# Attention inside a fused block: the order of the maxima and of the P·V products on TensorE is rewritten

## The reference

```
x = x + tanh(g_xattn) * linear(attn_text + attn_image)      # on layernorm(x)
    q = rms_norm(linear(x)); k = rms_norm(linear(ctx)); v = linear(ctx)
    attention(q, k, v) = softmax(q k^T / sqrt(32)) v         # 16 heads of 32
    # the context has 1344 text rows and 257 image rows; each has its own softmax
x = x + tanh(g_ffn) * (top-2 of 8 experts + shared expert)   # on layernorm(x)
```

## Time and profile before

| | |
|---|---|
| median of 3 runs | 1711.67 us |
| the profiled execution | 1710.61 us |
| its span, first to last instruction | 1709.1 us |
| PE busy | 1667.6 us, 98% of the span |
| DVE busy | 1185.1 us, 69% |
| ACT busy | 833.4 us, 49% |
| POOL busy | 901.4 us, 53% |
| granted TensorE clock, mean | 0.996 |

### The profile page before, as it was taken

The page is one execution under the profiler, slowest core; times in us unless marked ns, Lnnn a source line. Parts: engine busy times, 40 slices in busy tenths (PEclk is TensorE's granted clock), DMA queues, the critical chain, the costliest instruction groups (busy, mean ns, idle before and its releaser), DMA issues. The chain is left out here.

```text
span 1709.1 us, 24784 instructions
## 1 busy us (share of the span) xinstructions
PE 1667.6 (98%) x8694; PEld 1116.5 (65%) x8694; DVE 1185.1 (69%) x2220; ACT 833.4 (49%) x1550; POOL 901.4 (53%) x343
## 2 busy tenths in 40 slices
PE   6999999999999999999999999998999999999999
PEld 5888878886444455555555545445777778888777
DVE  6876677668888887888878888777444454443565
ACT  4443333326666664666556666662221355554221
POOL 3221311215777775788747777710515576775642
PEclk9999999999999999999999999999999999999999
DMA  9556858646555552565555655211314477885532
GB/s 331 169 159 195 241 173 208 197 150 196 152 155 156 146 153 66 154 159 157 139 136 147 158 135 140 93 48 42 136 38 157 167 258 262 269 273 197 174 103 99
DMA packets 198603, 277.34 MB, mean 162 GB/s; under 512 B 30968, under 2 KB 128008, under 8 KB 197964
## 3 DMA queue, kind: packets, MB, share of 16 engines
q1 hardware_dynamic: 192928, 258.91, 51.0%
q0 software_dynamic: 5120, 16.78, 2.9%
q10 hardware_dynamic: 432, 0.07, 0.0%
HBM read 202.21 MB, written 106.42 MB: 181 GB/s over the span
## 5 line engine op out<-in xcount | busy, mean ns | idle before, releaser
L1294 ACT ACTIVATE P<-ps 128x512 f32<-128x512 f32 (+1 forms) x832 | 445.2, 597 | 230.5 <-PE ps L1135 173.4
L1425 DVE TENSOR_REDUCE mp<-ps 128x1 f32<-128x448 f32 x720 | 397.1, 615 | 69.6 <-PE ps L1115 68.6
L1575 POOL TENSOR_TENSOR sacc<-sacc,P 128x2048 f32<-128x2048 f32 x90 | 397.9, 4421 | 16.4 <-ACT P L1294 5.5
L1115 PE MATMUL ps<-Kst,Qst 96*128 96x448 f32 (+1 forms) x960 | 338.2, 373 | 1.8 <-DVE stl L626 1.7
L1135 PE MATMUL ps<-Qst,Kst 100*128 100x512 f32 (+1 forms) x832 | 323.9, 413 | 3.5 <-ACT P L1294 2.6
L1115 PEld LDWEIGHTS ps<-Kst,Qst 96*128 96x128 f32 x960 | 182.7, 190 | 162.4 <-DVE mp L1425 99.1
L1069 PE MATMUL ps<-P,Vg 128*32 128x512 f32 (+2 forms) x1664 | 216.1, 606 | 0.3 <-ACT P L1294 0.2
L822 POOL TENSOR_TENSOR cl<-craw,ch 128x1024 fp32r<-128x1024 f32 (+2 forms) x26 | 61.8, 2378 | 283.0 <-ACT ch L550 283.0
L1135 PEld LDWEIGHTS ps<-Qst,Kst 100*128 100x128 f32 (+1 forms) x832 | 152.9, 186 | 67.4 <-ACT P L1294 38.5
L49 PE MATMUL ps<-W,ch 128*128 128x512 f32 (+1 forms) x408 | 162.5, 398 | 0.0
L51 PE MATMUL ps<-W,cl 128*128 128x512 f32 (+1 forms) x408 | 159.7, 391 | 0.0
(11 more groups left out here) (249 smaller groups left out, 3142.6 us busy)
## 6 DMA issues: line engine op xcount, KB each, us to landing
gur<-in_w_gate_up SPq DMA_DIRECT2D x23, 1024.0 KB, 7.3
Kst<-KHd SPq DMA_DIRECT2D x56, 320.0 KB, 4.7
Vd<-vf SPq DMA_DIRECT2D x50, 256.0 KB, 2.1
craw<-in_ctxT SPq DMA_DIRECT2D x24, 512.0 KB, 4.4
KHd<-sth SPq DMA_DIRECT2D x24, 512.0 KB, 3.4
KLd<-stl SPq DMA_DIRECT2D x24, 512.0 KB, 4.9
dnr<-in_w_down SPq DMA_DIRECT2D x23, 512.0 KB, 3.8
xg<-Xg SPq DMA_DIRECT2D x23, 512.0 KB, 7.9
```

The source lines that it names most:

```text
L1115: ins = pe.matmul(ps[:, bank, 0:c1 - c0], Qst[G % 3][0:96, j, 128 * qt:128 * qt + 128], Kst[s][0:96, j, c0:c1], start=True, stop=True)
L1294: act.activation(P[slot(G, kt)][:m, j, :], ps[:m, 2 + (e - 1) % 3, :], ACT.Exp, scale=SCALE).then_inc(a_exp, 1)
L1425: dve.reduce_max(out, ps[:, bank:bank + k, 0:cols] if k > 1 else ps[:, bank, 0:cols], AX.X).then_inc(d_ra, 1)
L1575: pool.tensor_tensor(sacc[:, h], sacc[:, h], P[slot(G, kt)][:, h], ALU.add).then_inc(g_sum, 1)
```

## The change

Three things change, all within the attention. The numbers of units in a step become 5, 6, 6, 6, 6, 6, 6, 5 in steps 3 to 10 (before: 6, 5, 6, 6, 6, 6, 5, 6); all other steps and the total of 64 stay. The order of the blocks becomes 21 long ones, then the 16 image units spread evenly among the remaining 27 long ones (before: 46 long ones, and then the 16 image units, nearly all together). And tiles 2 to 7 are weighed two to a run, in steps 5, 7 and 9, with none in steps 4, 6, 8 and 10; tile 8 goes into the run of step 11, which then has three tiles.

```
-    UNITS = (7, 6, 3, 6, 5, 6, 6, 6, 6, 5, 6, 2, 0)
+    UNITS = (7, 6, 3, 5, 6, 6, 6, 6, 6, 6, 5, 2, 0)
...
-    EVENTS = [(x,) for x in ORDER_MAX]
+
+    def mixed_order():
+        blocks = [(j, qt) for j in range(4) for qt in range(4)]
+        long = [(c, *x) for c in (0, 1, 2) for x in blocks]
+        image = [(3, *x) for x in blocks]
+        order, long = long[:21], long[21:]
+        for i in range(16):
+            k = (27 * i + 8) // 16, (27 * i + 35) // 16
+            order += long[k[0]:k[1]] if i else long[:k[1]]
+            order.append(image[i])
+        return order + long[(27 * 15 + 35) // 16:]
+
+    EVENTS = [(x,) for x in mixed_order()]
...
         def text_end(G):
+            weigh(G, 8, 0, 128, False, False)
             weigh(G, 9, 0, 128, False, False)
             weigh(G, 10, 0, 64, False, True)
...
-            if 3 <= kt < 11:
+            if kt == 3:
+                weigh(G, 1, 0, 128, False, False)
+            if kt in (5, 7, 9):
+                weigh(G, kt - 3, 0, 128, False, False)
                 weigh(G, kt - 2, 0, 128, False, False)
```

## The result

| | before | after |
|---|---|---|
| median (us) | 1711.01 (1708.58 to 1713.34, 6 runs) | 1718.47 (1716.88 to 1720.16, 6 runs) |
| ratio | | 1.0046, 95% interval 1.0035 to 1.0056 |
| span of the profiled execution | 1709.1 | 1716.9 |

The change makes the kernel 0.46% slower, 7.5 us. The prediction was 1712.4, with 1704 to 1720 as its range. The time lies inside, but it is 6.1 us above the point, and outside the 0.3% that count as the same. As a difference between the two kernels, 0.7 was forecast and 7.5 came: 6.8 more. The median of before is 0.7 lower over six runs than over the three that the forecast started from.

What follows compares the result with a forecast made beforehand. POOL's unbroken chain of adds was taken to bound ordinary groups, not busy PE. Terms +4.4 (ordinary), -3.8 (groups 5 and 9), +0.1 (group 15) gave +0.7: 1711.3 profiled, 1712.4 us as median, range 1704 to 1720.

Steps and rivals of the forecast that it cites:

- Ordinary groups, +0.34 each: 13 groups: the text run starts 0.50 us earlier but takes 0.86 longer, so each group grows 0.34, +4.4 in all.
- the wall: Ordinary groups, step 10: the exponential cannot start before POOL's add of tile 6 ends, whatever PE does faster in steps 4-9.
- PE has 2.14 less to do up to step 10: Ordinary groups: seven single runs become three pairs, tile 8 leaves; PE saves 7 x 1.18 - 3 x 2.04 = 2.14 us.
- The mixed order at nothing: Ordinary groups: spreading the image units and the new numbers of units cost nothing, since POOL's chain hides DVE.
- Groups 5 and 9, -3.8: Groups with projections: PE reaches the projection 2.14 us earlier, DVE's adds come 1.9 earlier; 2 x 1.9 = 3.8 less.
- Group 0, priced as an ordinary one: Group 0 was counted among the 13 ordinary groups, at +0.34 us.
- Group 15, +0.1: Last group, no units and no POOL: between -1.3 and +1.0 us, taken as +0.1 since DVE's chain hides both.
- DVE's add of tile 7: Ordinary groups: starts earlier, about 765.0, fully beside POOL's last add; the port lock makes it end near 766.42 again.
- B: Rival: the run behind the wall starts no earlier and ends 0.86 us later per ordinary group, total 1719.2; chance 0.15.
- A: Rival: PE sets the pace everywhere, so 16 groups save 1.28 us each, 20.5 less, total 1691.2; chance 0.08.
- C: Rival: DVE's add takes time from POOL, whose last add grows by 0.7 us; total 1717.8; chance 0.05.
- D: Rival: a group's end hangs on DVE's add of tile 8, starting 0.6 us earlier; total 1700.2; chance 0.06.

Runs made afterwards that it cites:

- experiment 3: The kernel after, but tile 8 weighed alone in step 10, so the text run has two tiles again: 1720.4 us, ratio 1.0048 to before.
- experiment 1: The kernel before with only the mixed block order and the new numbers of units, tiles weighed singly as before: 1712.15 us, ratio 1.0006.
- experiment 2: The kernel before with only the paired weighings and tile 8 in step 11, old block order and numbers of units: 1724.98 us, ratio 1.0088.
- experiment 6: The kernel after, with DVE's maxima taken over half the columns of each bank: 1729.41 us, ratio 1.0109 to the kernel before.
- experiment 5: The kernel before, with DVE's maxima taken over half the columns of each bank: 1708.32 us, ratio 0.9978.
- experiment 9: The kernel after, with DVE's statistics of projected tiles moved from groups 5 and 9 to groups 6 and 10: 1719.87 us, ratio 1.0053 to before.
- experiments 7 and 8: Kernels before and after, maxima over half the columns, POOL adding two of four heads of tiles 3 to 5: 1701.11 and 1682.33 us.

## Why the prediction was right, and where it was wrong

*Ordinary groups, +0.34 each: right, by the path behind the wall.* 0.36 on average, by the path that was written down: no gap in step 10, a run that starts 0.53 earlier (0.50 predicted), takes 2.92, and ends 5.46 behind the first exponential (5.4). POOL's adds took 27.21, the wait for POOL was there 25 times and 23.1 us. The add of tile 7 ended at 37.63 in the group, 37.62 before.

*But its premise, "PE has 2.14 less to do up to step 10", failed.* That PE's saving waits at the wall was read into the trace. In the kernel after there is no such stock: nothing is saved by the end of step 9, and experiment 3 puts a weighing back in front of the wall, gains nothing on the kernel after, and is still 0.4 behind the kernel before. What I had missed is the other engine in the middle. I priced the pair as PE time alone, and DVE as an average over two steps, 6.5 against 6.5, "about even". Both were wrong by size, 5.96 on PE and 5.4 on DVE, and an average can't see that 2.04 without a unit empties the ring, whose pause of 1.0 brings DVE's two steps to 6.47. The 69.6 us that DVE idles for PE between maxima, beside a PE that waits for banks of DVE 82 times in other places than behind a run, were the hint; I didn't follow it up.

*The mixed order at nothing, "POOL hides it".* Right with single runs (experiment 1), wrong with pairs (experiment 2 against the kernel after: 0.6 an ordinary group). I never priced one half of the change without the other. The cover that I named, POOL's wall, is gone in experiment 2.

*Groups 5 and 9, -3.8: wrong, the step that failed is "PE reaches that point 2.14 earlier".* It reaches it 0.30 later. From there on the chain was as I had put it: one long unit in place of an image unit adds 0.2, DVE's add of tile 7 and the third exponential behind it come 0.49 later, and the group is 0.49 longer. So the term's end was read rightly and its input not: +1.0 in place of -3.8, which is 4.8 of the 6.8 by which the forecast difference missed. With cheaper maxima the -1.9 appears (experiment 6 against 5), so the failure is DVE's lateness and not the price of a run.

*Group 0, priced as an ordinary one.* In the profiled execution it lost 1.7 more, of which 1.63 is the run at half clock. I had not asked what a longer wait of PE does to the clock. With the full clock (experiment 9) it loses 0.43, and the term was right.

*Group 15, +0.1: right by luck.* It takes 43.69 to the end of its text run against 43.60, but before's 43.60 holds the stretch at half clock. With the full clock the same work takes 42.31 (experiment 5), so the term was +1.4, above the +1.0 that bounded it. Why the pairs cost this group 1.4 was not followed up; "DVE's chain hides both" is not what happened. With 4.8 for groups 5 and 9, 1.3 here, and 0.1 and 0.3 in group 0 and the other ordinary ones, the miss comes to 6.4 at full clock, of the 6.8 between the medians; no low clock is needed to explain it.

*DVE's add of tile 7, "lies fully beside POOL's last add": it didn't.* I had it start 0.6 earlier, since the mixed order would let DVE finish earlier. It starts 0.16 later in the group (36.95, before 36.79), 0.05 before POOL's end, and takes the 0.68 that it takes alone. That it ends where I said is a coincidence, and this group says nothing of the lock. The traces of before and of experiments 5 and 6 do (last section), and they bear the lock out.

*The rivals.* B gave 1719.2, the nearest number, and not for the reason that made it so: the run does start earlier, and ordinary groups lose 0.36 and not 0.86. A is false of this kernel, since PE's saving does not arrive, and true of one with light DVE and POOL (experiments 7 and 8). C and D did not occur: POOL's adds kept their time, and the end followed the run.

What stays open: in how many of the six runs of each kernel group 0 or group 15 met the low clock (only the profiled ones show it); what decides whether PE's clock falls; why group 15 loses 1.4; why the pairs alone cost groups 5 and 9 so little; and what a lighter POOL alone would give.

## What to carry to other kernels

Work saved on the engine that seems to set the pace is saved only if its consumer can take the output in the new rhythm: for each lump of other work on the producer compare its length with what the consumer has in its buffers, not the averages of both over a step. When a change has two halves, price each alone and both together, since one may be worth nothing without the other. And before making an engine faster in front of a fixed wait, look at the wait that results, for PE's clock may fall behind it.

## What the hardware showed that I had not expected

**The granted clock fell to half behind short waits of PE.** After 1.51 us idle (group 0 after) and after 1.85 to 1.89 (most ordinary groups of experiment 6) it was at 0.50 to 0.51 in the run that followed, and the 24 records took 4.34 to 4.55 in place of 2.92. The length of the one wait doesn't decide it. In group 0 PE kept its clock after 0.68 (before), 0.87 (experiment 2) and 1.35 (experiment 9); in experiment 6 group 3 waited 1.85 and kept it, group 7 waited 1.89 and lost it. And in group 15, where PE has no units to do, it fell behind 0.47 before and stayed behind 0.48 after. PE before, with the clock of the stretch (the number behind the five engines), then PE after:

```profile
1112.99 1.78 PE L1135 MATMUL ps<-Qst,Kst 100*128 100x512 f32 x3 [0.47 <-ACT P L1294]
1114.70 2.89 PE L1069 MATMUL ps<-P,Vg 128*32 128x512 f32 x16
...
1113.30:1116.70 3.40, 3.40 (x15) 1.17 (x18) 3.24 (x2) 2.18 (x5) 0.00 (x0) 0.50 0.05 10
```

```profile
1119.69 1.48 PE L1147 MATMUL ps<-Qst,Kst 100*128 100x512 f32 x3 [0.48 <-ACT P L1310]
1121.10 1.92 PE L1081 MATMUL ps<-P,Vg 128*32 128x512 f32 x16
```

So groups of one kernel can differ by 1.6 us within an execution (45.8 and 47.5 in experiment 6), and a comparison of one group between two single traces can be off by as much: look at the clock of both first.

**DVE's add waits for POOL's, and for all of it.** DVE's add of tile 7 takes 0.68 us where POOL is idle (groups 5 and 9). In the 13 ordinary groups of the kernel before it starts 0.15 to 0.89 before the end of POOL's last add and ends 0.55 to 0.56 behind it each time, whatever its start (0.55 is 0.13 less than it takes alone). In experiments 5 and 6 it starts 0.62 to 1.05 before that end, takes up to 1.59, and again ends 0.55 to 0.56 behind it. POOL's add takes 3.45 to 3.50 in these groups, and 3.46 to 3.49 in experiments 7 and 8, where it has no such company. So DVE's add is held until POOL's is through, and POOL's loses nothing; if the two divided a bandwidth, POOL's add would get longer with the overlap and DVE's would not end at one fixed distance. The opposite order, with DVE first, doesn't occur here.
